# A graph layer's gathers: the last tile of 22 groups fetched row by row from SyncE and ScalarE instead of by GpSimd

## The reference

```
xn = layernorm(x);  xp = xn + xn @ Wpos + (degree term)
q, k, v = xp @ Wq, xp @ Wk, xp @ Wv                  # (n, H, D/H)
att = clip(sum(q[dst] * k[src]), -50, 50)            # per edge and head
alpha = softmax of att over the edges of each dst
aggr[dst] += v[src] * alpha                          # sum over edges
x = x + aggr @ Wo;  x = x + gelu(layernorm(x) @ W1) @ W2
```

## Time and profile before

| | |
|---|---|
| time, median of three runs (2790.19 to 2799.18) | 2799.0 us |
| span of the profiled execution, first to last instruction | 2183.8 us |
| the median less that span (the profiled execution has no time of its own) | 615.2 us |
| busy: VectorE, GpSimd, TensorE, ScalarE | 78%, 72%, 65%, 43% |
| instructions in the trace | 32409 |
| edge groups of layer 0, of layer 1 (gathers) | 98 to 1109 us, 1144 to 2154 us |

### The profile page before, as it was taken

The page is one execution under the profiler, slowest core; times in us unless marked ns, Lnnn a source line. Parts: engine busy times, 40 slices in busy tenths (PEclk is TensorE's granted clock), DMA queues, the critical chain, the costliest instruction groups (busy, mean ns, idle before and its releaser), DMA issues.

```text
span 2183.8 us, 32409 instructions
## 1 busy us (share of the span) xinstructions
PE 1419.8 (65%) x8227; PEld 1237.3 (57%) x8227; DVE 1710.2 (78%) x5103; ACT 940.2 (43%) x2179; POOL 1570.6 (72%) x1669
## 2 busy tenths in 40 slices
PE   4866576666667676766666657566666757666666
PEld 4555565656555565655556556556555656555555
DVE  8759888888877878787877777777777778777775
ACT  8334353534535353534454335343343435343344
POOL 6277777777777777777727777777777777777773
PEclk9979888877878788887988787787787778787787
DMA  2365445444444444444424444444444444444441
GB/s 87 119 178 182 148 133 154 147 136 134 142 134 125 142 134 142 124 142 134 132 69 143 135 125 136 137 123 139 133 139 124 139 134 129 134 134 138 125 138 56
DMA packets 123505, 289.29 MB, mean 132 GB/s; under 512 B 31525, under 2 KB 57057, under 8 KB 123329
## 3 DMA queue, kind: packets, MB, share of 16 engines
q0 software_dynamic: 77824, 212.31, 33.8%
q1 hardware_dynamic: 45504, 74.92, 10.3%
HBM read 275.44 MB, written 8.38 MB: 130 GB/s over the span
## 4 chain that ended last, share of the span: by engine, by line
POOL 47%; issue 20%; DVE 11%; PE 11%; DMA 6%; ACT 3%; DVEq 1%; SPq 0%; ACTq 0%
POOL kvr L801 47%; DMA kvr<-kv_table,srcidx 5%; PE bank L1079 4%; PE bank L1092 3%; DVE agg L1706 3%; DVE kvr L1322 2%; DVE prod L1675 1%; DVE msg L1697 1%; ACT apart L1279 1%; ACT onehotT L1283 1%; DVE onehot L1667 1%; PE bank L1036 1%; PE bank L1015 1%; PE bank L816 1%; PE bank L894 1%
## 5 line engine op out<-in xcount | busy, mean ns | idle before, releaser
L801 POOL DMA_INDIRECT kvr<-kv_table,srcidx x1612 | 1530.7, 950 | 547.4 <-issue 480.0
L1079 PE MATMUL bank<-q,onehotT 128*128 x3320 | 606.8, 340 | 712.1 <-DVE prod L1675 475.2
L1079 PEld LDWEIGHTS bank<-q,onehotT 128*128 128x128 f32 x3320 | 515.6, 237 | 825.5 <-issue 824.8
L1092 PE MATMUL bank<-msg,onehot 128*128 128x136 f32 x3320 | 612.3, 344 | 1.9 <-DVE msg L1697 1.9
L1289 ACT ACTIVATE bank<-attc 128x32 f32<-128x32 f32 x404 | 81.2, 201 | 1145.7 <-DVE attc L1691 1145.0
L1092 PEld LDWEIGHTS bank<-msg,onehot 128*128 128x128 f32 x3320 | 571.8, 252 | 3.6 <-DVE msg L1697 3.3
L1675 DVE TENSOR_TENSOR prod<-kvr,bank 128x512 f32<-128x512 f32 x404 | 276.0, 683 | 302.6 <-DMA kvr<-kv_table,srcidx 264.0
L1706 DVE TENSOR_TENSOR agg<-agg,bank 128x136 f32 x1624 | 469.1, 289 | 44.9 <-PE bank L1092 40.1
L1279 ACT ACTIVATE apart<-relT,minus_p 128x512 bf16<-128x512 bf16 x416 | 293.8, 706 | 4.4 <-DMA relT<-rel_table 4.0
L1667 DVE TENSOR_TENSOR onehot<-bank,rel 128x512 f32<-128x512 f32 x416 | 282.5, 682 | 0.2
L1697 DVE TENSOR_TENSOR msg<-kvr,bank 128x512 f32<-128x512 f32 x404 | 273.9, 678 | 5.0 <-ACT bank L1289 4.9
(11 more groups left out here) (217 smaller groups left out, 844.5 us busy)
## 6 DMA issues: line engine op xcount, KB each, us to landing
relT<-rel_table SPq DMA_DIRECT2D x104, 512.0 KB, 4.1
kvr<-kv_table,srcidx POOLq DMA_INDIRECT x1612
loop_kv<-kv_table SPq DMA_DIRECT2D x25, 128.0 KB, 3.9
kv_table<-qkv SPq DMA_DIRECT2D x25, 128.0 KB, 3.2
kv_table<-onehot SPq DMA_DIRECT2D x8, 256.0 KB, 2.2
w<-weights SPq DMA_DIRECT2D x2, 840.0 KB, 7.4
loops<-x_in SPq DMA_DIRECT2D x5, 320.0 KB, 5.6
q<-qkv SPq DMA_DIRECT2D x25, 64.0 KB
```

The lines of the kernel that those rows point to most:

```text
L801: pool.indirect_dma_start(kvr[:, n % RING, j, :], None, kv_table[l], bass.IndirectOffsetOnAxis(ap=srcidx[:, step:step + 1], axis=0)).then_ ...
L1079: mm = pe.matmul(bank[2][:, j * D:(j + 1) * D], onehotT[:, m % OHT, j, :], q[:, bass.ds(ranks[j + h], 1), :].rearrange("p a c -> p (a c)") ...
L1092: mm = pe.matmul(sum_ps(n, k), onehot[:, m % OH, j, :], msg[:, n % 2, j, :], start=(m, j) == of[0], stop=(m, j) == of[-1])
```

## The change

Eleven groups a layer (31, 47, ... 191) leave their last tile out of GpSimd's gathers. The 128 rows of such a tile are fetched one by one by ordinary DMAs with the node's number in a register, half of them by SyncE, half by ScalarE: in each of the 16 slots g - 22 to g - 7 ahead of group g each of the two loads four node numbers from `srcrow` and issues four DMAs of one row, 2 x 512 B, to `rowkv`, one of two buffers. The first slot of a tile also waits until its buffer is free and the table is complete. VectorE does the product and the message of such a group in two instructions, three tiles from `kvr` and one from `rowkv`, with one more wait ahead of the second. `srcrow` is copied once, near the start, by 11 DMAs on SyncE, behind a new wait for the step tables (`s_rows`) ahead of the wait at L614.

```diff
+ROWED = tuple(range(31, 192, 16))
+ROWS_A_SLOT, ROWS_LEAD, ROW_BUFS = 8, 6, 2
+ROWS_SP = 4
+ROW_SLOTS = P // ROWS_A_SLOT
...
+def pooled(n):
+
+    return gathers(n) - is_rowed(n)
...
+        def fetch_tile_rows(engine, which, l, g, part, first_row, rows):
+
+            i = rowed_no(l * GROUPS + g)
+            if part == 0:
+                if i >= ROW_BUFS:
+                    before = (i - ROW_BUFS) // len(ROWED) * GROUPS + ROWED[(i - ROW_BUFS) % len(ROWED)]
+                    engine.wait_ge(s_msg, before + 1)
+                engine.wait_ge(s_srcrow, 16 * len(ROWED))
+                if l == 0:
+                    engine.wait_ge(s_first_table, 16 * len(KV_PAIRS))
...
+            p0 = part * ROWS_A_SLOT + first_row
+            at = ROWED.index(g) * P + p0
+            nodes = nc.values_load_multi_w_load_instructions(srcrow[0:1, at:at + rows], engines=(which,), min_val=0, max_val=NP - 1,
...
+            for j, node in enumerate(nodes):
+                engine.dma_start(rowkv[p0 + j:p0 + j + 1, i % ROW_BUFS, :, 0:D], kv_table[l][bass.ds(node, 1), :].rearrange("a (h c) -> a h c", h=2)).then_inc(s_rowkv[i % ROW_BUFS], 16)
...
+            sp.wait_ge(s_rows, 16 * 2 * SC)
+            for i, g in enumerate(ROWED):
+                chunk, step = divmod(row_of(g, at_begin=True) + G - 1, P)
+                sp.dma_start(srcrow[0:1, i * P:(i + 1) * P], step_src[step:step + 1, chunk * P:(chunk + 1) * P]).then_inc(s_srcrow, 16)
...
+                    for g in ROWED:
+                        if 0 <= s - (g - ROWS_LEAD - ROW_SLOTS) < ROW_SLOTS:
+                            fetch_tile_rows(sp, ENG.SP, l, g, s - (g - ROWS_LEAD - ROW_SLOTS), 0, ROWS_SP)
...
-                for j in range(gathers(n)):
+                for j in range(pooled(n)):
...
+                    for g in ROWED:
+                        if 0 <= s - (g - ROWS_LEAD - ROW_SLOTS) < ROW_SLOTS:
+                            fetch_tile_rows(act, ENG.Activation, l, g, s - (g - ROWS_LEAD - ROW_SLOTS), ROWS_SP, ROWS_A_SLOT - ROWS_SP)
                     dense_parts(l + 1, s)
...
+                t = pooled(n)
+                ins = dve.tensor_tensor(prod[:, 0:t, :], kvr[:, n % RING, 0:t, 0:D], bank[2][:, 0:t * D].rearrange("p (j c) -> p j c", c=D), ALU.mult)
+                if is_rowed(n):
+                    i = rowed_no(n)
+                    dve.wait_ge(s_rowkv[i % ROW_BUFS], 16 * P * (i // ROW_BUFS + 1))
+                    ins = dve.tensor_tensor(prod[:, t, :], rowkv[:, i % ROW_BUFS, 0, 0:D], bank[2][:, t * D:(t + 1) * D], ALU.mult)
```

More of the change, by code:

```diff
@@ L168, in is_seam, with is_rowed, rowed_no @@
     return n % GROUPS < SEAM_GROUPS
+def is_rowed(n):
+    return n % GROUPS in ROWED
+def rowed_no(n):
+    return n // GROUPS * len(ROWED) + ROWED.index(n % GROUPS)
+def pooled(n):
+    return gathers(n) - is_rowed(n)
 def row_of(n, at_begin=False):
@@ L201, in landed @@
 def landed(n):
-    return 16 * sum(gathers(k) for k in range(n % RING, n + 1, RING))
+    return 16 * sum(pooled(k) for k in range(n % RING, n + 1, RING))
 def blocks_by(c):
@@ L329, in build @@
         kvr = sb("kvr", [P, RING, G, KV])
+        rowkv = sb("rowkv", [P, ROW_BUFS, 2, D + 4])
+        srcrow = sb("srcrow", [1, len(ROWED) * P], I32)
         onehot = sb("onehot", [P, OH, G, P])
@@ L504, in build @@
         s_kv = [sem(f"s_kv{r}") for r in range(RING)]
+        s_srcrow = sem("s_srcrow")
+        s_rowkv = [sem(f"s_rowkv{u}") for u in range(ROW_BUFS)]
         s_oh = sem("s_oh")
@@ L597, in read_perm @@
                                                             skip_runtime_bounds_check_because="the number of the block that has a rank")[1]
+        def fetch_tile_rows(engine, which, l, g, part, first_row, rows):
[7 more added lines that the diff above has]
+                    engine.wait_ge(s_first_table, 16 * len(KV_PAIRS))
+                else:
+                    for u in range(2):
+                        c = NCH - 1 - u
+                        engine.wait_ge(s_table[buffer(l, c)], stored(l, c))
+            p0 = part * ROWS_A_SLOT + first_row
+            at = ROWED.index(g) * P + p0
+            nodes = nc.values_load_multi_w_load_instructions(srcrow[0:1, at:at + rows], engines=(which,), min_val=0, max_val=NP - 1,
+                                                             skip_runtime_bounds_check_because="the number of a node")[1]
+            for j, node in enumerate(nodes):
+                engine.dma_start(rowkv[p0 + j:p0 + j + 1, i % ROW_BUFS, :, 0:D], kv_table[l][bass.ds(node, 1), :].rearrange("a (h c) -> a h c", h=2)).then_inc(s_rowkv[i % ROW_BUFS], 16)
         program = ctx.enter_context(nc.Block())
@@ L1673, in edge_prod @@
                 dve.wait_ge(s_qe, n + 1)
-                t = gathers(n)
-                dve.tensor_tensor(prod[:, 0:t, :], kvr[:, n % RING, 0:t, 0:D], bank[2][:, 0:t * D].rearrange("p (j c) -> p j c", c=D), ALU.mult).then_inc(s_prod, 1)
+                t = pooled(n)
[4 more added lines that the diff above has]
+                    ins = dve.tensor_tensor(prod[:, t, :], rowkv[:, i % ROW_BUFS, 0, 0:D], bank[2][:, t * D:(t + 1) * D], ALU.mult)
+                ins.then_inc(s_prod, 1)
             def edge_att(n):
@@ L1695, in edge_msg @@
                 dve.wait_ge(s_ex, n + 1)
-                t = gathers(n)
-                dve.tensor_tensor(by_head(msg[:, n % 2, 0:t, 0:D]), by_head(kvr[:, n % RING, 0:t, D:KV]),
-                                  ex[:, 0:t * H].rearrange("p (j h) -> p j h", h=H).unsqueeze(3).broadcast_to([P, t, H, HD]), ALU.mult).then_inc(s_msg, 1)
+                t = pooled(n)
+                ins = dve.tensor_tensor(by_head(msg[:, n % 2, 0:t, 0:D]), by_head(kvr[:, n % RING, 0:t, D:KV]),
+                                        ex[:, 0:t * H].rearrange("p (j h) -> p j h", h=H).unsqueeze(3).broadcast_to([P, t, H, HD]), ALU.mult)
+                if is_rowed(n):
+                    ins = dve.tensor_tensor(msg[:, n % 2, t, 0:D].rearrange("p (h d) -> p h d", d=HD), rowkv[:, rowed_no(n) % ROW_BUFS, 1, 0:D].rearrange("p (h d) -> p h d", d=HD),
+                                            ex[:, t * H:(t + 1) * H].unsqueeze(2).broadcast_to([P, H, HD]), ALU.mult)
+                ins.then_inc(s_msg, 1)
             def edge_add(n, j, ranks):
```

1 line of the change is left out of this document (added).

## The result

The change makes the kernel slower: 3076.45 us (3063.3 to 3088.83, four runs) against 2798.07 (2790.19 to 2799.18, four runs), a ratio of 1.1005 with a 95% interval of 1.0969 to 1.1040. The forecast was 2773.4 us, and the range ended at 2900.

A forecast was written before the change was run, and what follows sets the result against it. GpSimd's gathers were taken to bound the kernel: -27.6 us for 22 gathers removed and +2 us for ScalarE's heavy slots make -25.6 us, from 2799.0 to 2773.4 us. The range was 2764 to 2900 us.

The forecast's parts named there:

- What bounds the kernel: Whole kernel: GpSimd's gathers, 1.254 us each, set the pace; VectorE has 8% slack in layer 0, 19% in layer 1.
- What is removed: GpSimd's queue: 11 tiles a layer, 22 gathers of 1.254 us off the pacing engine, -27.6 us.
- ScalarE: ScalarE's queue, slots 9 to 184: a piece takes 2.42 us, 1.79 new a slot, mostly fits; +2 us booked.
- SyncE, cost 0: SyncE's queue: the same 2.42 us piece in each 5.02 us slot, covered by lead and waits, cost 0.
- DMA engines, cost 0: DMA engines: 5632 more packets of 512 B, 445 us of one engine's time, GpSimd's pace untouched, cost 0.
- the far end: Upper price for ScalarE's row DMAs, from copies inside SBUF: 0.91 us a DMA, 3.93 us a piece; not taken.
- VectorE: VectorE's split product and message in 22 groups: 3.4 us a layer, covered by slack; uncovered +6.8 us in all.
- 1 (ScalarE becomes the bound): ScalarE's queue, slots 9 to 184: new time per slot passes 2.68 us; up to +190 us, 2989 us; chance 0.20.
- One of its signs: ScalarE's queue: its DMAs over 0.75 us apart would show that ScalarE has become the bound.
- 2 (the two queues hinder each other): ScalarE's and SyncE's DMAs wait for each other: some 2780 us, or 2936 if in every slot; chance 0.08.
- 3 (layer 0 gives nothing): Layer 0: heavy ScalarE slots bunch up, VectorE ends late by all of its 13.8 us gain; 2789 us; chance 0.12.
- 4 (time around the span): Outside the profiled span: the 615.2 us grow with 6336 more instructions, +120 us at most, 2894 us; chance 0.06.

The follow-up runs named there:

- 2 x 16 B: Changed kernel with 2816 DMAs from fixed rows, each two runs of 16 B into one partition, VectorE using a constant: 3104.15 us, 1.092 times before.

## Why the prediction was wrong

- *What bounds the kernel*: "GpSimd sets the pace from start to end of each layer" held for the execution of the earlier trace rows alone. In the timed ones a gather comes every 1.62 us and GpSimd waits 605.5 us for VectorE. The warning was on the page: a span of 2183.8 us against a time of 2799.0. "615.2 us lie around the span, which I leave as they are" was the first step that failed: they lie inside, the span of the same kernel being 2792.0 when timed.
- *What is removed*: -27.6 us. Right in sign, about half of the size: 60 us without rows (45 with the loads kept), each of one execution. The forecast's way to it (22 x 1.254) is not shown by that; why 22 gathers are worth 2.7 us each here was not split further.
- *ScalarE*: "This term decides", 0.53 us a DMA, 2.42 a piece. Measured 0.725 from one DMA to the next and 4.0 a piece, at the median, with the stops in it. Mis-sized, and not what decided: with pieces of 2.4 us from fixed rows the loss is all there, and SyncE's half alone costs as much as ScalarE's.
- *SyncE, cost 0*, and *DMA engines, cost 0*: this is the step that failed and that turned a gain into the loss. A DMA was priced by the queue that issues it and by its packets. The kernel pays about 0.1 us of its whole time for each DMA that has two runs in one partition, from either queue: 2816 x 0.11 = 310 us, more than the 278 lost. The row that the forecast set aside as the far end, three DMAs into one partition in ten runs at 717 ns, was nearer to this form than the single-run rows that it took.
- *VectorE*: 3.4 us a layer under cover. Nothing contradicts it; not tried alone.
- *Rivals*: 1 (ScalarE becomes the bound) came out on the right side for another reason. One of its signs came in part: 37% of the distances between its DMAs are over 0.75 us. The other, ScalarE's wait for VectorE falling to nothing, did not: its exponential waits 712.3 us for VectorE in the change and 1476.2 with 2 x 16 B. 2 (the two queues hinder each other) covers at most the 48 us that both halves cost over their sum; the Trainium skill's rule of the shared block (Perfetto Trace Analysis, DMA Instruction — HWDGE) is not contradicted, but no lock wait shows in the medians: a DMA takes 569 ns on ScalarE with SyncE issuing as well and 569 without, 568 and 567 on SyncE. 3 (layer 0 gives nothing) was never reached. 4 (time around the span) is excluded by 1.7 to 1.8 us in all runs. The Trainium skill (Runtime: NRT & Kernel Launch, The launch sequence) gives 9 to 15 us for a launch; what is measured here around the span is less, and how much of a launch the measured time takes in, no run shows.

## What to carry to other kernels

Compare the span of a profile with the timed runs before reading anything from it; where they are as far apart as here (2183.8 and 2799.0 us), the bound that it shows may not be the bound that is timed. Take the price of a DMA from one of the same form, and as the distance from one to the next. When rows are fetched one by one, give each DMA a single contiguous run in its partition: the padding of 4 elements between the halves made this change lose 10% instead of 0.9%. Even then the row DMAs cost what the 22 saved gathers gave (0.984 before them, 1.0087 with them), so here the gathers stay on GpSimd.

## What the runs showed of the hardware that was not expected

- A DMA from DRAM into one partition takes 566 ns to issue as two runs of 16 B and 265 ns as one run of 16 B or 512 B; into four partitions 636 ns with two or eight runs each, 317 with one.
- The dearer form slows engines that have nothing to do with it: 0.1 us of the kernel's time for each, the same from either queue, with 32 B and with 1 KB. For DMAs of 4 KB into four partitions it is 0.08 to 0.10, out of a total of 58 to 69 us.
- 45056 packets of 16 B in 2816 DMAs cost no more than 2816 packets in as many DMAs (0.994 against 1.001 times before).
- The same program ran in 2183.8 us of span in one execution and in 2792.0 in another, with 214 gaps on VectorE of 4.2 us on average in the second, one each 13 us; the mean granted clock of TensorE was 0.810 in the one and 0.684 in the other.
